# The end of the last batch reordered: three gate pairs and a down product behind the last scores, six PSUM banks in turn there, the last norm in halves

## Time and profile before

| what | value |
|---|---|
| median of three runs | 954.82 us (953.11 to 960.5) |
| profiled execution | 955.83 us, span 954.1 us |
| TensorE (PE) busy | 848.8 us, 89% of the span |
| VectorE (DVE) busy | 478.6 us, 50% |
| ScalarE (ACT) busy | 455.7 us, 48% |
| GpSimd (POOL) busy | 227.4 us, 24% |
| granted TensorE clock, mean over the span | 0.969 of full speed |

### The profile page before, as it was taken

How to read it: one execution, slowest core, us unless ns; L and a number is a source line. 1 busy time by engine, 2 the same in 40 slices (tenths; PEclk the granted TensorE clock), 3 DMA queues, 4 the chain that set the end, 5 groups by cost and what they waited for, 6 DMA issues and landing times.

```text
span 954.1 us, 15450 instructions
## 1 busy us (share of the span) xinstructions
PE 848.8 (89%) x6146; PEld 412.9 (43%) x6146; DVE 478.6 (50%) x1020; ACT 455.7 (48%) x721; POOL 227.4 (24%) x265
## 2 busy tenths in 40 slices
PE   4389998899989999899988999899988998999764
PEld 3144354443644446344544436344453434444332
DVE  2844346535455426645465355555275353545343
ACT  2255644555445554546445453555546453555211
POOL 0011131223212132122312232132321223231312
PEclk9599999999999999999999999999999999999968
DMA  6831443140511433113431406104321214100000
GB/s 211 213 97 45 89 89 111 45 90 23 141 59 45 111 66 107 72 43 70 89 111 45 89 23 152 70 23 111 82 74 45 64 48 109 47 1 23 1 22 24
DMA packets 44346, 71.09 MB, mean 75 GB/s; under 512 B 3568, under 2 KB 21232, under 8 KB 44272
## 3 DMA queue, kind: packets, MB, share of 16 engines
q1 hardware_dynamic: 44272, 70.07, 28.0%
HBM read 53.28 MB, written 16.78 MB: 73 GB/s over the span
## 4 chain that ended last, share of the span: by engine, by line
PE 73%; ACT 9%; DVE 9%; issue 4%; POOL 3%; DMA 2%; SPq 0%; POOLq 0%; ACTq 0%; DVEq 0%
PE ctx_ps L717 14%; PE misc L752 13%; PE den_ps L717 12%; PE slot L695 11%; PE misc L762 9%; PE misc L671 7%; PE misc L729 6%; ACT probs L409 6%; POOL work L364 2%; PE misc L680 2%; DVE work L548 2%; DVE x L531 1%; ACT work L421 1%; DVE ctx_raw L480 1%; DMA query_stack<-phi_dram 1%
## 5 line engine op out<-in xcount | busy, mean ns | idle before, releaser
L409 ACT ACTIVATE probs<-slot 128x1024 f32<-128x1024 f32 (+3 forms) x384 | 290.3, 808 | 376.4 <-PE slot L695 376.2
L695 PE MATMUL slot<-query_stack,key_stack 128*128 128x512 f16 (+3 forms) x768 | 161.7, 333 | 16.5 <-DMA query_stack<-phi_dram 15.1
L717 PE MATMUL ctx_ps<-probs,vz_sb 128*32 128x512 f32 (+3 forms) x1536 | 166.3, 505 | 10.3 <-DVE ctx_raw L480 8.3
L364 POOL TENSOR_TENSOR work<-work 128x512 f16<-128x512 f32 x96 | 112.7, 1174 | 216.0 <-ACT work L427 215.9
L717 PE MATMUL den_ps<-probs,ones 128*32 128x512 f32 (+3 forms) x1536 | 162.8, 495 | 0.0
L355 POOL TENSOR_SCALAR_AFFINE_SELECT probs<-probs 128x512 f32<-128x512 f32 x128 | 81.8, 641 | 303.9 <-ACT probs L409 302.9
L548 DVE SCALAR_TENSOR_TENSOR work<-work,misc 128x512 f32<-128x512 f32 x96 | 65.8, 686 | 172.7 <-ACT work L421 172.7
L752 PE MATMUL misc<-x1T_hi,w_parts 128*128 128x512 f16 x384 | 147.0, 383 | 5.2 <-DVE x1T_lo L538 2.4
L752 PE MATMUL misc<-x1T_lo,w_parts 128*128 128x512 f16 x384 | 146.5, 382 | 0.0
L695 PEld LDWEIGHTS slot<-query_stack,key_stack 128*128 128x128 f16 x768 | 56.8, 98 | 170.4 <-issue 120.9
L762 PE MATMUL misc<-w_parts,work 128*128 128x256 bf16 x768 | 89.1, 273 | 10.6 <-POOL work L364 10.6
(11 more groups left out here) (52 smaller groups left out, 609.8 us busy)
## 6 DMA issues: line engine op xcount, KB each, us to landing
key_stack<-phi_dram SPq DMA_DIRECT2D x64, 256.0 KB, 5.8
query_stack<-phi_dram SPq DMA_DIRECT2D x64, 256.0 KB, 6.5
xT_sb<-in_xT_dram SPq DMA_DIRECT2D x8, 1024.0 KB, 5.1
x_sb<-in_x_dram SPq DMA_DIRECT2D x8, 1024.0 KB, 5.5
out_dram<-x SPq DMA_DIRECT2D x16, 512.0 KB, 2.9
phi_dram<-phi_hi SPq DMA_DIRECT2D x16, 256.0 KB, 2.0
phi_dram<-phi_lo SPq DMA_DIRECT2D x16, 256.0 KB, 2.3
work<-in_wgT_dram SPq DMA_DIRECT2D x1, 768.0 KB, 8.2
```

The source lines that it names most:

```text
L364: pool.tensor_tensor(hid_lo[:, n % M1, :], hid[:, n % HSLOTS, :], hid_hi[:, n % M1, :], ALU.subtract).then_inc(hid_lo_ready, 1)
L409: act.activation(probs[:, s % P_SLOTS, 2 * p:2 * p + 2, off:CH], slot[p][:, :, off:CH], ACT.Exp).then_inc(slot_drained[p], 1)
L695: mm = pe.matmul(slot[p][:, k, off:CH], key_stack[:, h, P * j:P * (j + 1)], query_stack[:, h, CH * c + off:CH * (c + 1)], start=True, stop ...
L717: mm = pe.matmul(sums[32 * k:32 * k + 32, off:CH], w, probs[:, s % P_SLOTS, k, off:CH], start=first, stop=final)
```

## The change

The list of the last batch is written anew. From slot 18 on each gate pair gets two slots: pair 1 lies in slot 19, pair 2 in slot 21, their halves in slots 20 and 22. The list ends at slot 23, and `ending()` follows it: the three last weighs, with gate pair 3 between that of step 21 and that of step 22, then `normalise`, gate pairs 4 and 5 with their halves, `project` and the norm's statistics of chunk 1, `down(7, 0, 0)`, the norm's `apply`, the turn, `down(7, 0, 1)`, and then gate pairs 6 to 11. The final norm of chunk 0 lies among these: its statistics behind pair 8, its `apply` and its store behind pair 9. The final norm of chunk 1 is cut into two halves of two tiles, each with its own statistics, power, apply and store, and the first half's `apply` stands ahead of the second half's `ffn_residual` in VectorE's queue.

From `ending()` on, products take turns in six banks: the two `misc` and the four banks of the scores. The first product in a scores bank waits until the last exponentials have drained it. No arithmetic is changed; two halves take two 128x2 powers where one 128x4 was, and one store more.

```diff
+    LAST_BETWEEN = {
+        17: gate_pair(0, 0) + [("apply", 1, -1, 1), ("store", -1, 1)],
+        18: halves(0, 0),
+        19: gate_pair(0, 1),
+        20: halves(0, 1),
+        21: gate_pair(0, 2),
+        22: halves(0, 2),
+        23: [],
+    }
+
+    def ending():
+
+        b = B - 1
+        return ([("weigh", b, NS - 3)] + gate_pair(b, 3) + [("weigh", b, NS - 2), ("weigh", b, NS - 1)] + halves(b, 3)
+                + [("normalise", b, NQ - 1)] + gate_pair(b, 4) + halves(b, 4) + gate_pair(b, 5) + halves(b, 5)
+                + project(b, 1) + norm(0, b, 1) + down(b, 0, 0) + [("apply", 0, b, 1)]
+                + turn_x1(b, 1) + down(b, 0, 1)
+                + gate_pair(b, 6) + gate_pair(b, 7) + halves(b, 6) + gate_pair(b, 8) + halves(b, 7)
+                + norm(1, b, 0) + gate_pair(b, 9) + halves(b, 8) + [("apply", 1, b, 0), ("store", b, 0)]
+                + gate_pair(b, 10) + halves(b, 9) + gate_pair(b, 11) + halves(b, 10) + halves(b, 11)
+                + [step for s in range(2) for step in down(b, 1, s)
+                   + [("stats_half", b, 1, s), ("apply_half", b, 1, s), ("store_half", b, 1, s)]])
...
-        for what, *n in BETWEEN[i]:
+        for what, *n in (LAST_BETWEEN if b == B - 1 and i in LAST_BETWEEN else BETWEEN)[i]:
...
-        if LAG <= s < B * NS + LAG:
+        if LAG <= s < B * NS - 1:
...
-    SLOTS_ALL = (B + 1) * NS
     PLAN = first_projections()
-    for s in range(SLOTS_ALL):
+    for s in range(B * NS):
         PLAN += attention(s)
+    ENDING = len(PLAN)
+    PLAN += ending()
...
-    MISC, misc_uses = {}, [0, 0]
-    for what, *n in PLAN:
+    MISC, misc_uses, turn = {}, [0] * 6, 0
+    for at, (what, *n) in enumerate(PLAN):
         if what in ("scale", "vz", "turn_f", "project", "turn_x1", "gate", "up", "down"):
-            k = len(MISC) % 2
+            k = turn % (2 if at < ENDING else 6)
             MISC[(what, *n)] = (k, misc_uses[k])
             misc_uses[k] += 1
+            turn += 1
...
+        misc += [slot[n][:, k, :] for n in range(2) for k in range(2)]
...
+            def store_half(b, c, s):
+                sp.wait_ge(ln_done, TC * len(NORM) + 2 * (s + 1))
+                tiles = slice(TC * c + 2 * s, TC * c + 2 * s + 2)
+                sp.dma_start(out_v[b, :, tiles, :], x1[:, tiles, :]).then_inc(out_stored[c], 16)
...
+            def rsqrt_half(b, c, s):
+                pool.wait_ge(var_ready, len(NORM) + s + 1)
+                cols = slice(2 * s, 2 * s + 2)
+                pool.tensor_tensor(rstd[:, cols], var_eps[:, cols], neg_half[:, cols], ALU.pow).then_inc(rstd_ready, 1)
...
+            def stats_half(b, c, s):
+                done = len(NORM)
+                k, n = MISC["down", b, c, s]
+                dve.wait_ge(misc_drained[k], n + 1)
+                if s == 0:
+                    dve.wait_ge(ln_done, TC * done)
+                for t in (2 * s, 2 * s + 1):
+                    dve.bn_stats(bn[:, t, :], x1[:, TC * c + t, :]).then_inc(bn_ready, 1)
+                dve.wait_ge(bn_ready, TC * done + 2 * (s + 1))
+                for t in (2 * s, 2 * s + 1):
+                    dve.bn_aggr(mv[:, t, :], bn[:, t, :]).then_inc(mv_ready, 1)
+                dve.wait_ge(mv_ready, TC * done + 2 * (s + 1))
+                dve.tensor_scalar(var_eps[:, 2 * s:2 * s + 2], mv[:, 2 * s:2 * s + 2, 1], EPS, None,
+                                  ALU.add).then_inc(var_ready, 1)
+
+            def apply_half(b, c, s):
+                dve.wait_ge(rstd_ready, len(NORM) + s + 1)
+                for t in (2 * s, 2 * s + 1):
+                    row = x1[:, TC * c + t, :]
+                    dve.tensor_scalar(row, row, mv[:, t, 0:1], rstd[:, t:t + 1],
+                                      ALU.subtract, ALU.mult).then_inc(ln_done, 1)
...
                 if n >= 1:
                     pe.wait_ge(misc_drained[k], n)
+                elif k >= 2:
+
+                    pe.wait_ge(slot_drained[(k - 2) // 2], B * NS)
                 return k
```

More of the change, by code:

```diff
@@ L235, in seq_postln_kernel @@
         scale_ready = sem("scale_ready")
-        misc_filled = [sem(f"misc{n}_filled") for n in range(2)]
-        misc_drained = [sem(f"misc{n}_drained") for n in range(2)]
+        misc_filled = [sem(f"misc{n}_filled") for n in range(6)]
+        misc_drained = [sem(f"misc{n}_drained") for n in range(6)]
         slot_filled = [sem(f"slot{n}_filled") for n in range(2)]
@@ L335, in _ @@
                     store(*n)
+                elif what == "store_half":
+                    store_half(*n)
             for c in range(NC):
-                sp.wait_ge(out_stored[c], 16 * B)
+                sp.wait_ge(out_stored[c], 16 * (B + (c == NC - 1)))
         @block.gpsimd
@@ L371, in _ @@
                     rsqrt(*n)
+                elif what == "stats_half":
+                    rsqrt_half(*n)
                 elif what == "hid_lo":
@@ L641, in _ @@
                     apply(*n)
+                elif what == "stats_half":
+                    stats_half(*n)
+                elif what == "apply_half":
+                    apply_half(*n)
                 elif what == "split_x1":
```

## The result

The changed kernel takes 945.05 us (median of 7 runs, 942.77 to 949.1), the kernel before 953.15 us in the same series. The ratio is 0.9906, 95% interval 0.9877 to 0.9935: 9.0 us faster, between 6.2 and 11.7. The forecast was 945.5, or 9.3 us saved. Medians in this document are of all timed runs; one run of the kernel before (2175.61 us) and one of e6_filler (962.21 us) were in a slow state and enter no ratio.

The account below looks back on a forecast made before the run. TensorE bounds the slots until the last weigh, then the path goes from engine to engine. Savings 8.3 + 2.1 + 2.4 - 1.2 - 2.3 = 9.3 us take 954.82 to 945.5 us; 8-in-10 range 941.0 to 949.5.

Parts of the forecast that it names:

- Step 1: Slot 18 to the last weigh: one gate pair, two down products and a GpSimd wait removed, saving 8.3 us.
- Rival (b): Slots 20 and 22: scores wait for ScalarE's exponentials, 3.4 us of the saving go, 948.9 us; chance 0.13.
- Step 2: Last weigh to gate pair 6: gate 6 starts 10.4 us earlier, the 8.3 us saved before it included.
- Step 3: Gate pairs 6 to 11: with six banks VectorE is the bound, 16.2 us to the down product, a gain of 2.4.
- the `apply`, 1.33: Among gate pairs 6 to 11: chunk 0's final-norm `apply` on VectorE was to take 1.33 us.
- Step 4: Tail, chunk 1's down product to the end: 15.2 us, 1.2 more than before, with 2.1 lost to low clock.
- The clock in the new holes: Three new TensorE holes, in slot 18 and around `down(7, 0, 0)`: lower clock behind them costs 2.3 us, bounds 0 and 5.1.
- Rival (a): The clock never falls in the new gaps and is up early in the last down: 941.1 us; chance 0.07.
- (d): The clock stays low from the first hole to gate pair 6, making the kernel slower, up to 977 us; chance 0.04.
- (c): Down products and pairs taken out had hidden waits that now show in full; time stays 954.8 us; chance 0.05.

Follow-up runs that it names:

- e6_filler: Changed kernel with 24 products that nobody reads behind gate pair 11, filling TensorE's idle time before the last down product; 945.24 us, ratio 0.9906 to the kernel before.
- e1: Changed kernel with the ending taking turns in the two misc banks only instead of six; 950.71 us, ratio 0.9947 to the kernel before.
- e2: Changed kernel with the last norm of chunk 1 in one piece, one apply and one store; 948.33 us, ratio 0.9926 to the kernel before.
- e5: Changed kernel with the final norm of chunk 0 moved behind the halves of pair 11; 942.01 us, ratio 0.986 to the kernel before.
- e9: Changed kernel with products that nobody reads in all four TensorE holes (9, 8, 8 and 24); 940.86 us, ratio 0.9856 to the kernel before.
- e4: Changed kernel with gate pair 1 back in slot 18 under the `ctx_ps` wait, its halves in slot 19; 944.63 us, ratio 0.9879 to the kernel before.
- e8: Changed kernel with pair 1 in slot 18, chunk 0's final norm behind pair 11, tanh 5 before pair 4's halves, apply before `ffn_residual`; 935.95 us.
- e7: Changed kernel, as a probe, with GpSimd computing only 16 of 512 columns of the low half for hidden tiles 8 and 9; 946.0 us.
- e3: Changed kernel with gate pairs 1 to 5, two down products and chunk 0's final norm at their old places, six banks and halved norm kept; 949.86 us.
- e10: The e8 kernel with 12 products that nobody reads behind gate pair 11; 933.71 us, ratio 0.9783 to the kernel before.

## Why the prediction was right

- **Step 1, 8.3 us: right.** Before, the last weigh ended 30.5 us behind the copy in slot 18 (901.65 - 871.16). At full clock it is 21.9 (e1, e2, e5, e6, e9), 8.6 less. That pair 1 was free where it stood and costs 1.7 us behind the wait is shown by e4. Rival (b), ScalarE in the thin slots, is out: between the weigh at 870.42 and the last one TensorE is never idle for over 0.1 us, so no scores waited for exponentials.
- **Step 2: right to 0.4 us.** Gate 6 was forecast 10.4 us earlier. From the copy in slot 18 to gate 6 (at 910.73) it is 50.3 us before (921.46 - 871.16) and 41.1 after: 9.2 less, and 10.8 without the 1.65 us of low clock behind slot 18, which the forecast counts apart. Both orders that the forecast named as holding it up (tanh 5 behind `hid_hi` 4, `apply` behind `ffn_residual`) gave 1.8 us together when turned around (e8).
- **Step 3: the step's mechanism held, one term was mis-sized.** From gate 6 to the down product it was 16.2 forecast and 17.4 measured (928.16 - 910.73), so these pairs gained 1.2 us and not 2.4. The term "the `apply`, 1.33" took 2.87, because two of its four instructions waited out GpSimd's `hid_lo` (e7). VectorE is the bound there, and six banks are what makes it so (e1, e5).
- **Step 4: 15.2 forecast, 14.6 measured.** The low-clock down half was 4.95 (4.9), the halves 3.5 and 3.6 (3.6). The rest is the last store: 2.6 us from its issue to the end, where 3.05 stood in the sum.
- **The clock in the new holes, 2.3 us: the right size for the mean.** Each fall costs 1.6 to 1.7 us. In the six traces for each hole that have it unfilled and unchanged the clock fell behind slot 18 in two of six, behind the project in two of six, and behind `down(7, 0, 0)` in five of six, nine of eighteen where four in seven was assumed: 2.5 us for three holes. The profiled execution had one fall in them, 1.65. e9 removes all: 4.8 us by the ratios, of which 2.1 are the last hole, so 2.7 for the three, give or take 3. Rival (a), no falls, is out; so is (d), as no fall lasted: the clock was at full again before gate pair 6 each time.
- **Luck.** That the total came out 0.4 us from the forecast is in part luck. The pairs saved 1.2 us less than forecast; the tail (0.6), step 2 (0.4) and, in this one trace, the clock (0.65) made up for it.
- **The chances.** The median gain was 0.94%, and its interval straddles the 1% on which the forecast was split. (c), the filler was free, is out: with the old places back (e3) the path is 4.2 us longer by the traces, 3.9 by the ratios.

## What to carry to other kernels

Before moving work from behind a barrier to fill idle time later, look at what it covered: work under a wait of another engine is free, and taken away it leaves a hole that costs its length only if it was on the path, but may cost the clock as well. Where the last stretch of a kernel is a chain through all engines, cut the traces at fixed instructions and compare the stretches, and count the falls of the clock in each: runs of 945 us that differ by 6 us hide edits of 2 us, the stretches repeat to 0.01, and one fall more in one of two traces is as large as a small edit. Once one engine's stalls are gone, put what is not urgent on the new bound (here a norm on VectorE) where that engine waits.

## What was not expected of the hardware

- **A VectorE `apply` that meets GpSimd's work waits for the end of it.** The `apply` instruction on a 128x256 tile in SBUF takes 0.40 or 0.41 us. In the twelve traces 116 of 1536 took from 0.7 to 1.3 us, and every one of the 116 ended 0.14 to 0.15 us behind the end of a GpSimd instruction (a `hid_lo` of 1.16 us or a `mask` of 0.64). Eight of them stand in the trace of the kernel before, so this could have been read there. The `hid_lo` lost next to nothing (1.16 and 1.20 us). The `hidden` instructions, one input of which lies in PSUM, kept their 0.75 us beside it (916.60 beside GpSimd's 916.44). The Trainium skill (VectorE: DVE Perf Modes, "Mode 2×_2P — use both read ports for one tensor" and "Two Vector instructions with no wait between them") says that such one-tensor operations read SBUF through both of the lane's ports, and that the second is shared with GpSimd; e7 agrees, 1.37 against 2.87 us for four.
- **Equal holes, different clocks.** A hole of 3.22 or 3.23 us ahead of the last down product left full clock twice (the kernel before, e3) and the lower level twice (e5, e8: 5.3 and 4.4 us for a first half of 2.8), and a hole of 2.12 us could be enough (e4, e7), even one of 1.96 (e1). Holes of 1.58 to 1.73 us (one each in e6, e8, e9 and e10) were followed by no fall. The Trainium skill (TensorE: Matmul & The Clock Gate, "Why this matters for your kernels") asks only that gaps longer than those of 2.1 to 2.5 us be avoided. Nine falls behind eighteen holes of 2.1 to 2.4 us disagree with it, and they decide.
- **Half the columns, less time for the power.** GpSimd's power took 0.70 us on 128x2 and 1.01 on 128x4, so a half norm gains 0.3 us more than its VectorE part.
